# Three score buffers to five, and one weight load moved ahead of the first activations, in an eight-core attention layer

## What is computed

```
q = x@Wq + bq            16 heads of 64
k, v = x@Wk + bk, x@Wv + bv     2 heads of 64, each shared by 8 query heads
scores of a token: its 256-wide window (128 back, 127 ahead); zeros past the ends
a = softmax(scores) @ v,  then a@Wo + bo
x = layernorm(x + a)
r = sigmoid((mu_r*x + (1-mu_r)*x_prev) @ W_r^T)
k2 = relu((mu_k*x + (1-mu_k)*x_prev) @ W_k^T)^2
x = layernorm(x + r * (k2 @ W_v^T))
```

## Time and profile before

| what | us |
|---|---|
| median of 2 runs | 1062.5 (1062.02 to 1062.99) |
| the profiled execution: its own time | 1058.03 |
| its span on the slowest core (core 1), first to last instruction | 1056.5 |
| spans of the eight cores | 1045.1 to 1056.5 |

### The profile page before, as it was taken

One profiled execution on the slowest core, in us unless ns is written; L12 is line 12 of the kernel. 1 busy time (PEld: TensorE's weight loads), 2 busy tenths in 40 slices (PEclk: granted clock), 3 DMA queues, 4 the chain that ended last, 5 costly groups with the idle time before them and its releaser, 6 DMA issues. The chain is left out here.

```text
span 1056.5 us, 11399 instructions; the slowest of 8 cores (1045.1 to 1056.5 us)
## 1 busy us (share of the span) xinstructions
PE 603.1 (57%) x2834; PEld 227.2 (22%) x2834; DVE 315.0 (30%) x735; ACT 262.7 (25%) x720; POOL 96.7 (9%) x101
## 2 busy tenths in 40 slices
PE   0077556612666665565667655564328678586682
PEld 0033222201222221221222212121103223232230
DVE  0021112101332322323232233333160834617405
ACT  0011000501332322332333233231003032141332
POOL 2000000100000000000000000000033306024030
PEclk9998778655666666666666666666559889897996
DMA  9945642797323233333233333323330040030201
GB/s 111 148 73 85 105 64 41 102 169 152 73 63 76 65 67 74 76 70 65 65 69 77 60 80 66 66 65 66 63 61 0 21 100 11 40 90 0 80 1 80
DMA packets 178142, 75.05 MB, mean 71 GB/s; under 512 B 165920, under 2 KB 166048, under 8 KB 178080
## 3 DMA queue, kind: packets, MB, share of 16 engines
q1 hardware_dynamic: 165248, 48.37, 23.1%
q0 software_dynamic: 12832, 25.96, 13.8%
HBM read 43.01 MB, written 8.39 MB: 49 GB/s over the span
## 5 line engine op out<-in xcount | busy, mean ns | idle before, releaser
L503 ACT ACTIVATE p<-psc,konst 128x384 bf16<-128x384 f32 x272 | 155.3, 575 | 354.6 <-PE psc L491 343.6
L571 PE MATMUL po<-pt,vt 128*64 128x128 bf16 x408 | 63.3, 289 | 184.3 <-DMA pt<-p16n 184.1
L485 PE MATMUL psc<-maskq,ident 128*128 128x384 bf16 x272 | 106.0, 426 | 35.0 <-ACT p L503 30.1
L608 PE MATMUL pwo<-w16o,ao 128*128 128x512 bf16 x272 | 102.9, 546 | 22.4 <-DVE ao L591 22.4
L868 PE MATMUL pr<-w16r,xr 128*128 128x512 bf16 x256 | 67.5, 427 | 58.9 <-DVE xk L846 32.4
L591 DVE CAST ao<-po 128x512 bf16<-128x512 f32 x34 | 23.5, 692 | 243.5 <-PE po L576 243.5
L931 PE MATMUL pr<-w16vf,kact 128*128 128x512 bf16 x256 | 67.5, 431 | 32.9 <-DVE g L945 19.9
L571 PEld LDWEIGHTS po<-pt,vt 128*64 128x64 bf16 x408 | 36.0, 141 | 219.9 <-issue 219.9
L297 PE MATMUL paP<-xfm,w16k 128*128 128x512 bf16 x40 | 17.9, 626 | 96.5 <-DMA xfm<-x16t 96.5
L530 DVE TENSOR_SCALAR p16n<-p,rall 128x384 bf16<-128x384 bf16 x272 | 65.4, 309 | 0.1
L576 PE MATMUL po<-pt,vt 128*64 128x128 bf16 x408 | 64.9, 293 | 0.0
(11 more groups left out here) (68 smaller groups left out, 563.1 us busy)
## 6 DMA issues: line engine op xcount, KB each, us to landing
x<-xpad POOLq DMA_DIRECT2D x17, 512.0 KB, 4.0
out<-out SPq DMA_DIRECT2D x16, 512.0 KB, 2.7
x16t<-xpad POOLq DMA_DIRECT2D x5, 1024.0 KB, 10.7
pt<-p16n SPq DMA_TRANSPOSE x136, 2.8
w16q<-wq POOLq DMA_DIRECT2D x1, 2048.0 KB, 36.7
w16o<-wo POOLq DMA_DIRECT2D x1, 2048.0 KB, 19.1
w16r<-wr POOLq DMA_DIRECT2D x1, 2048.0 KB, 31.4
w16kf<-wkf POOLq DMA_DIRECT2D x1, 2048.0 KB, 45.4
```

The lines of the kernel that those rows point to most:

```text
L485: e.matmul(psc[:, HH % 3, 0:WIN], ident[:, :], maskq[:, :], start=True, stop=False)
L503: e.activation(p16[:, tau % 2, h, :], psc[:, H % 3, 0:WIN], AF.Exp, bias=konst[:, 0:1], accum_out=sall[:, h:h + 1]).then_inc(bEX.sem, 1)
L571: last = e.matmul(po[0:64, slot * 128:(slot + 1) * 128], lhs, pt16[:, slot_a, c * 128:(c + 1) * 128], start=(c == 0), stop=(c == 2), tile_ ...
L608: e.matmul(pwo[:, nh * 512:(nh + 1) * 512], ao16[:, tau % 2, kc, :], w16o[:, kc, nh * 512:(nh + 1) * 512], start=(kc == 0), stop=False)
```

## The change

Two edits. The first moves the issue of `w16q` and `bo` ahead of both batches of activations in GpSimd's row; the separate early call of `load_xbatch(0)` goes, since the loop over groups makes it anyway. The second gives `psc` five buffers in place of three: the head number is taken modulo 5, and a mask matmul of head `HH` waits for `HH-4` exponentials where it waited for `HH-2`. With that, block B holds all 8 banks of PSUM.

```
+        v_wq = g_dma(w16q[:, :, :], wq_in.ap().rearrange("(c p) n -> p c n", p=128))
+        v_bo = g_dma(bo16[:, :], bo_in.ap())
         wlate = [
...
-        load_xbatch(0)
-        v_wq = g_dma(w16q[:, :, :], wq_in.ap().rearrange("(c p) n -> p c n", p=128))
-        v_bo = g_dma(bo16[:, :], bo_in.ap())
...
-        nc.psum_tensor("psc", [128, 3, 512], F32) as psc,
+        nc.psum_tensor("psc", [128, 5, 512], F32) as psc,
...
-                            if HH >= 3:
-                                e.wait_ge(bEX.sem, HH - 2)
-                            e.matmul(psc[:, HH % 3, 0:WIN], ident[:, :], maskq[:, :],
+                            if HH >= 5:
+                                e.wait_ge(bEX.sem, HH - 4)
+                            e.matmul(psc[:, HH % 5, 0:WIN], ident[:, :], maskq[:, :],
                                      start=True, stop=False)
...
-                    e.matmul(psc[:, H % 3, 0:WIN],
+                    e.matmul(psc[:, H % 5, 0:WIN],
...
-                    e.activation(p16[:, tau % 2, h, :], psc[:, H % 3, 0:WIN], AF.Exp,
+                    e.activation(p16[:, tau % 2, h, :], psc[:, H % 5, 0:WIN], AF.Exp,
```

## The result

The changed kernel takes 1037.4 us (median of 11 runs, 1032.93 to 1040.86) against 1062.81 before (10 runs). The ratio is 0.9766, with a 95% interval of 0.9738 to 0.9794.

The account below looks back on a forecast made before the run. No engine is full; a ring of hand-overs in block B bounds the kernel. −13.5 − 7.5 − 4.0 + 0.7 = −24.3 from a median of 1062.5 gives 1038.2 us, 8-in-10 range 1030 to 1051.

Parts of the forecast that it names:

- The logarithm's place: Block B's layer norm: with five buffers ACT reaches the logarithm 0.9 us sooner in 15 iterations, −13.5 us.
- The clock in `wo`: In block B's `wo` matmuls, shorter iterations make early clock rises frequent: 0.5 us in each of 15, −7.5 us.
- two kinds: `wo` groups in block B: late clock rise, taking 7.20 us, or early rise, taking 5.70 us.
- the ring: Block B's regular iteration as a chain of hand-overs from `wo` through DVE, ACT, transposes and p·v to `wo`: 30.63 us.
- The head start in iteration 0: Block B's start: exponentials without gaps finish 4.7 us sooner, and the fourth transpose follows; taken as −4.0 us.
- The moved weight: Kernel start: `w16q` ahead of the activations shifts the first transposes, +0.7 us on the slowest core, bounds −2 and +4.
- 1 (no help from the clock, 1045.7): Block B: chain shortens by 0.9 us but clock rises shift with it or jump as rarely; 1045.7 us, chance 0.25.
- 2 (buffers off the ring): Block B: clock or SP's transposes keep the pace at 30.6 us, only the start gains; 1059 us, chance 0.12.
- for 3: Block B: the clock rise in `wo` fails in most iterations, making the kernel slower; 1091 us, chance 0.03.
- the masks' wait: Sign in block B: TensorE's wait for ACT at the mask matmuls falls to near nothing.
- the pace: Sign in block B: spacing of GpSimd's issues, one per iteration, becomes 29.2 us.
- The test on p·v of pair 3: Sign at block B's start: p·v of pair 3 starts near 249 us.

Follow-up runs that it names:

- the early logarithm: Kernel before, three buffers, with the layer norm's two ACT instructions queued earlier, so four exponentials and not six stand ahead of the logarithm: 1027.44 us, ratio 0.9717.
- the logarithm held back: Kernel before with five score buffers and two idle ACT activations put between the sixth exponential and the logarithm: 1046.63 us, ratio 0.9879.
- the held-back logarithm: Kernel before, three buffers kept, with two idle ACT activations put ahead of the logarithm: 1062.38 us, ratio 1.0007.
- The runs with pieces: Kernel before with block C's three weights loaded in 24 pieces along block B's iterations: five buffers 1012.68 us (0.9559), three buffers 1023.34 us (0.9683).

## Why the prediction was right

It said 1038.2, and 1037.4 was measured. The direction and the two large terms rest on the right mechanism. That the number is within 1 us is partly luck, since errors of both signs cancelled. Term by term, against the rows of after:

- *The logarithm's place*, −13.5: right in mechanism and nearly in size. 0.91 us was worked out from the earlier trace rows, 1.02 measured, −15.3 in 15 iterations. Four experiments bear it: five and four buffers give the same 4.01 us; the early logarithm gives more without buffers; both together give no more than it alone.
- *The clock in `wo`*, −7.5: right in mechanism, sized somewhat high. `wo` fell by 0.39 a time where 0.5 was taken, −5.9. Over all eight cores it fell by 0.28 (6.66 to 6.38), −4.2. The mean on core 0 is 6.51, near the 6.45 of an even spread, but the mean before was 6.90 and not 7.2: the rise moves through `wo` by degrees (5.85, 6.42 and 6.90 us in the first three of the 14 groups) and does not only jump between two kinds. Nor are 5.70 and 7.20 the ends of the scale, as the groups of 4.1 to 4.4 us with the logarithm held back show. That the old pace could not be held with less work in the ring is borne out by the alternating paces and, from the other side, by the held-back logarithm that cost nothing. The rises 30.7 us apart, whether `wo` starts 29.35 or 31.74 us behind the one before, show it directly. The rule of the Trainium skill, page "TensorE: Matmul & The Clock Gate", section "What's actually happening", that the counter behind the clock runs free of the kernel, agrees with these rows.
- *The head start in iteration 0*, −4.0: this term failed. The step that failed is "starting 4.7 us sooner therefore brings the fourth transpose some 4.7 us sooner". The share of packets is still nearly equal (405 and 442 in 5 us after, before), but it is small until the weights have landed and large behind that: on core 0 after, the transposes move 405 packets in the 5 us from 245 and 2917 in the 5 us from 255. The end of the loads is not moved by the head start (58.4 us behind the first matmul before, 58.2 after), so p·v of pair 3, near that end, gained 1.7 us as a mean, p·v of pair 4, behind it, 0.6, and the first `wo` 0.9. The runs with pieces show the same on a smaller scale with `w16o`.
- *The moved weight*, +0.7: within what can't be measured. The cores scatter by 5 to 7 us in their first k matmul in either order; by itself the edit gave 0.9990 (0.9972 to 1.0007).

So the sum of the first three was −25.0, and −15.3 − 5.9 − 0.9 = −22.1 is what the rows give. Block B starts 1.5 us later on core 0 after than on core 1 before (192.15 and 190.70), which makes −20.6, and the two profiled executions, from which all rows come, differ by 19.8 (1058.03 and 1038.19). The medians differ by 25.4. So the rows account for the profiled executions, and 5 to 6 us of the medians' difference are how far the executions lie from their medians: 1058.03 is 4.8 below the median before, 1038.19 is 0.8 above that after. A sum that had the third term right would have said about 1041.3. The rivals: 1 (no help from the clock, 1045.7) and 2 (buffers off the ring) are ruled out by the cuts and by the held-back logarithm; for 3 there is no sign, the mean clock of the slowest core rose from 0.738 to 0.741. The profile's tests came out as named for the masks' wait, the logarithm (3.34, named 3.45) and the pace (29.27, named 29.2). The second reciprocal comes 4.9 us sooner behind the first matmul (4.7 in the sum), and the first k matmul is at 54.6 on core 1, and at 54.2 on core 7, where it was 51.1. The test on p·v of pair 3 (named 249, 250.9 on core 0, which started 1.5 us later) looked right by chance: core 1 before was the latest of the eight there, 62.5 us behind its first matmul with a mean of 60.3, and core 0 after is at 58.7. As a mean only 1.7 us were gained.

## What to carry to other kernels

A wait of the busiest engine is worth what it delays on the ring of hand-overs, not its length: here 30 us of TensorE's waiting for buffers stood in a hole anyway, and what counted was one small instruction of ACT in a queue behind work nobody was waiting for. Before adding buffers, try to queue that instruction earlier; here it gave more and cost no memory. Here transposes that were issued sooner within a load that filled the DMA engines were through hardly sooner at its end. Taking the load apart and spreading it over the iterations gave more than the whole change, though some pieces still met a transpose.

## What the runs showed that I had not expected

The time need not follow the work. With 0.8 us added to the chain of each iteration it stayed the same (1.0007); with 0.2 us taken off (the held-back kernel with five buffers) it fell by 1.2%, as `wo` went from 6.66 to 5.94 us as a mean over the cores. The rows show a granted clock that rises inside `wo` at moments 30.7 us apart, which do not move along with `wo`. An iteration that is a little longer or shorter meets the rise earlier or later in its `wo`, and the pace stays near 30.7 us; beyond a range of chain lengths it is lost, and rises 27.3 us apart come in between. What sets these two distances no run here shows. A small edit tried on such a kernel can measure as nothing and still be real, or measure at several times its size.
